# A causal attention kernel whose first pair of heads per batch goes up the blocks of queries, with the near pieces of its bias table loaded during the projections

## The chip, the cores and the metric

The kernel runs on one core of one Trainium2 chip. The metric is the device time of one execution in microseconds (us); lower is better. The engines are called as in the profile: PE (TensorE, matrix multiply; PEld is its weight load), DVE (VectorE), ACT (ScalarE), POOL (GpSimd) and SP (SyncE, which issues most of the DMAs here; SPq is its queue).

## The reference, cut to what matters

Two batches of 2048 tokens with 512 features go through one attention layer with 16 heads of 64 that share one key and one value head, and then through a feed-forward layer with ternary weights. Only the attention matters for the change:

```python
q = l2norm((xn @ Wq) per head) * q_scale
k = l2norm(xn @ Wk) * k_scale            # one key head for all 16
sim = 8.0 * q @ k.T + bias[i - j]        # relative position bias from a small network
sim = where(j <= i, sim, -inf)           # causal; a null key with its own bias stays visible
out = softmax(sim) @ [null_v, v]
```

Everything is held to float32 accuracy by splitting values into a high and a low half of 16 bits.

## The kernel before, in words

Each batch has three stages, written for every engine as `project`, `attend` and `output`. In `project` the 16 tiles of 128 tokens go through a pipeline of stages with lags: normalise, split, turn by DMA (`turn_x`), multiply by the weights on PE (L1255), square, sum, root, scale (`b_unit`, L1020, writes `qn`), take the high half on ACT (`b_high`, L716) and the low half on POOL (`b_low`, L562), and turn the pair of halves by DMA into `qT` (`turn_q`, L420). Keys and values take a shorter way: `b_turn_k` (L1267) turns the keys of a tile on PE, and `b_keys` on ACT (L727) copies them into `kT`; `b_turn_v`, `b_vhigh` and `b_values` (L1041) make the values. `output` of the first batch overlaps the first steps of the second batch's `project`.

`attend` works on 8 pairs of heads (`hp`). In a pair the queries are cut into 4 blocks `i` of 512, and a unit is a block `i` with a tile `j` of 128 keys, `j` from 0 to 4i+3: 4, 8, 12 and 16 units, `NU` = 40 in all. The last four units of a block lie on the diagonal and are 4, 3, 2 and 1 quarters wide. `BLOCKS` is 3, 2, 1, 0, so every pair goes down: block 3 with its 16 units first. Each unit goes through these engines in order:

- PE, `score` (L1286, L1289): 4 matmuls of up to 512 columns into two of four PSUM banks, so unit k waits until unit k-2 is biased.
- DVE, `bias` (L1058): scale, add the bias table, write `probs`, a ring of 10 (`RING`).
- ACT, `exps` (L749): Exp in place.
- POOL, `low_part` (L577): the low half, a ring of 8 (`LRING`). Units with `j` = 3 off the diagonal (3 of 40, `WHOLE`) have no low part; they are weighed in float32 (L1308).
- PE, `weigh` (L1322): multiplies probabilities with values into sums, in three parts that come 6, 8 and 9 slots behind `score` (`LAG`, `LATE`).

At a block's end ACT makes the null key's part (`null_part`, L756, 8 instructions), DVE drains the three sums (`drain`, L1077, L1079; its first part waits for the null part), and ACT stores the result (`store_o`, L765, 8 instructions). When these come is set by the dictionaries `NULLS`, `DRAINS` and `STORES`, by slot.

The bias table of a pair sits in `tab`, two heads of 2048 columns, loaded from DRAM in four pieces of 512 columns (L436), each waiting for the landing of the one before. Block `i` tile `j` reads 512 columns from 512i - 128j on, so block 3 begins with piece 3 and soon needs piece 2, and block 0 needs piece 0 alone. `tab` is shared with the projections' buffers: pieces 0 and 1 lie where `x_re` (the output stage's reload of x) and `xhl` (the split input of `turn_x`) are, pieces 2 and 3 where `x_in` and `xT` are. `probs`, `low` and `null_tmp` share `work` with the projections' `rest`, `sq`, `khl`, `qn` and `qhl`.

Order around the change: each engine's instructions stand in one stream. On PE, `attend` comes behind `b_turn_k` of the last tile and begins with waits for all keys, all values, `b_pn` and all of `turn_q`. On SP, `attend` comes behind the last `turn_q`. On ACT, `attend` begins with the Exp of `p_null` (L781), which loads the Exp table of functions, and `b_pn` then lets POOL begin.

## Time and profile before

| | us |
|---|---|
| median of 3 runs | 1564.64 |
| lowest, highest | 1559.87, 1564.86 |
| the profiled execution's own time | 1564.24 |
| its span in the trace | 1562.5 |
| mean granted TensorE clock | 0.971 |

The profiled execution is 0.40 us under the median, and 1.74 us of it lie outside the span. Busy shares of the span are PE 92%, PEld 60%, DVE 77%, ACT 67% and POOL 81%. The share is a mean over stages: in the forty slices of the page POOL is at 9 tenths or more through the attention of both batches and at 4 to 7 in the other stages.

### The profile page before, as it was taken

The numbers are of one execution on the slowest core, as the hardware profiler recorded it, in microseconds if no ns is written. First come the engines' busy times: TensorE is split into PE (matmuls) and PEld (weight loads), VectorE is DVE, ScalarE is ACT, GpSimd is POOL, SyncE is SP. The second block draws the span as 40 slices with busy tenths as digits, with TensorE's granted clock in tenths as the row PEclk, the third lists the DMA queues.
The fourth block names the chain that finished last, engine by engine and source line by source line (L and its number), as shares of the span: only waits on it lengthen the run. The fifth ranks groups of instructions, "written<-read, shape, count | busy, mean of one in ns | idle before, by whom it ended". The sixth has DMA issues, their size and how long they took to land.

```text
span 1562.5 us, 39526 instructions
## 1 busy us (share of the span) xinstructions
PE 1434.3 (92%) x13844; PEld 935.6 (60%) x13844; DVE 1199.8 (77%) x2071; ACT 1041.8 (67%) x2140; POOL 1262.5 (81%) x908
## 2 busy tenths in 40 slices
PE   4888995999999999997997995999999999997996
PEld 2444552777777777774443552777777777776442
DVE  4455885788788788784997885788888888886797
ACT  4664654889888888886112563788888888888110
POOL 4564755999999999997653663999999999999553
PEclk9999996999999999998999997999999999999998
DMA  7003874111211201201885885111111121110796
GB/s 213 1 1 72 176 146 84 44 27 42 47 24 42 48 23 42 51 6 30 173 189 142 159 164 105 41 42 42 29 42 42 29 42 42 29 29 5 143 192 148
DMA packets 225620, 114.93 MB, mean 74 GB/s; under 512 B 193200, under 2 KB 193712, under 8 KB 225456
## 3 DMA queue, kind: packets, MB, share of 16 engines
q1 hardware_dynamic: 220864, 104.42, 31.9%
q10 hardware_dynamic: 4608, 8.39, 1.5%
q8 instruction: 110, 1.80, 0.5%
q14 instruction: 38, 0.31, 0.1%
HBM read 58.11 MB, written 8.54 MB: 43 GB/s over the span
## 4 chain that ended last, share of the span: by engine, by line
PE 58%; POOL 11%; issue 9%; DVE 7%; DMA 3%; ACT 2%; SPq 1%; DVEq 0%; POOLq 0%; ACTq 0%
PE ps L1322 15%; PE ps L1286 12%; PE ps L1289 11%; PE ps L1255 10%; POOL work L577 7%; PE ps L1361 4%; PE ps L1308 4%; DVE work L1058 4%; POOL work L590 2%; DMA work<-work 1%; DMA tab<-bias_table 1%; POOL work L607 1%; SPq L452 1%; DVE work L1077 1%; PE ps L1370 1%
## 5 line engine op out<-in xcount | busy, mean ns | idle before, releaser
L577 POOL TENSOR_TENSOR work<-work 128x1024 f16<-128x1024 f32 (+3 forms) x592 | 932.6, 1624 | 28.5 <-ACT work L749 28.5
L1058 DVE SCALAR_TENSOR_TENSOR work<-ps,tab 128x1024 f32<-128x1024 f32 (+3 forms) x640 | 668.5, 1057 | 171.6 <-PE ps L1289 140.1
L749 ACT ACTIVATE work<-work 128x1024 f32<-128x1024 f32 (+3 forms) x640 | 572.9, 922 | 157.5 <-DVE work L1058 152.9
L1322 PEld LDWEIGHTS ps<-vals,work 128*128 128x128 bf16 (+1 forms) x7936 | 435.4, 99 | 108.6 <-POOL work L577 6.7
L1322 PE MATMUL ps<-vals,work 128*128 128x129 f16 (+1 forms) x7936 | 460.8, 207 | 4.0 <-POOL work L577 3.1
L1286 PE MATMUL ps<-qo,kT 128*128 128x512 f16 (+3 forms) x1280 | 345.5, 352 | 30.3 <-DVE work L1058 15.9
L1289 PE MATMUL ps<-qo,kT 128*128 128x512 f16 (+3 forms) x1280 | 344.6, 351 | 0.0
L1289 PEld LDWEIGHTS ps<-qo,kT 128*128 128x128 f16 x1280 | 123.4, 99 | 119.3 <-issue 6.3
L1361 PE MATMUL ps<-wout,work 128*128 128x512 f16 x768 | 174.0, 385 | 18.2 <-DMA work<-work 18.2
L1255 PE MATMUL ps<-wq,tab 128*128 128x512 f16 x768 | 177.3, 381 | 0.4
L1361 PEld LDWEIGHTS ps<-wout,work 128*128 128x128 f16 x768 | 75.9, 99 | 111.7 <-DMA work<-work 18.4
L765 ACT ACTIVATE qo<-work,rec 128x64 f32 (+1 forms) x512 | 128.4, 333 | 3.5 <-DVE rec L1082 3.5
L756 ACT ACTIVATE work<-null_v,p_null 128x65 f32<-128x65 f32 x512 | 128.7, 334 | 0.0
L797 ACT CAST work<-qo 128x1024 f16<-128x1024 f32 x32 | 33.4, 1045 | 138.3 <-DMA work<-work 138.2
L1255 PEld LDWEIGHTS ps<-wq,tab 128*128 128x128 f16 x768 | 74.8, 101 | 78.0 <-issue 2.7
L1286 PEld LDWEIGHTS ps<-qo,kT 128*128 128x128 f16 x1280 | 84.8, 99 | 47.9 <-DVE work L1058 30.9
L1308 PE MATMUL ps<-vals_w,work 128*128 128x65 f32 x768 | 109.1, 275 | 0.0
L1308 PEld LDWEIGHTS ps<-vals_w,work 128*128 128x128 f32 x768 | 100.6, 192 | 6.6
L598 POOL TENSOR_TENSOR rstd<-ve,minus_half 128x1 f32<-128x1 f32 x32 | 17.5, 548 | 82.6 <-DVE ve L1116 82.6
L590 POOL TENSOR_TENSOR work<-qo,work 128x1024 f16<-128x1024 f32 x32 | 68.0, 2126 | 12.5 <-ACT work L797 12.5
L1077 DVE TENSOR_TENSOR work<-ps,work 128x195 f32<-128x195 f32 (+1 forms) x192 | 63.1, 329 | 18.2 <-PE ps L1322 17.8
L567 POOL TENSOR_TENSOR tab<-tab 128x512 f16<-128x512 f32 x32 | 37.0, 1157 | 47.7 <-ACT tab L682 47.7
(135 smaller groups left out, 1276.3 us busy)
## 6 DMA issues: line engine op xcount, KB each, us to landing
tab<-bias_table SPq DMA_DIRECT2D x64, 512.0 KB, 4.6
tab<-in_x SPq DMA_DIRECT2D x64, 256.0 KB, 3.1
out_x<-work ACTq DMA_DIRECT2D x32, 256.0 KB, 2.3
work<-in_L_cond_Wq SPq DMA_DIRECT2D x1, 2048.0 KB, 8.7
work<-in_L_cond_Wout SPq DMA_DIRECT2D x2, 1024.0 KB, 10.2
qo<-in_L_cond_w SPq DMA_DIRECT2D x1, 1024.0 KB, 7.3
work<-work SPq DMA_TRANSPOSE x64, 4.3
qo<-in_L_cond_b SPq DMA_DIRECT2D x2, 256.0 KB, 5.4
```

The source lines that it names most:

```text
L577: pool.tensor_tensor(low[:, k % LRING, :, c0:512], probs[:, r, :, c0:512], high[:, r, :, c0:512], ALU.subtract).then_inc(low_pool, 1)
L590: pool.tensor_tensor(o_hl[:, u, 1, :].rearrange("p (h d) -> p h d", d=DH), o_all[:, :, tile, :], o_hl[:, u, 0, :].rearrange("p (h d) -> p ...
L749: act.activation(probs[:, k % RING, :, c0:512], probs[:, k % RING, :, c0:512], ACT.Exp).then_inc(expd, 1)
L756: last = act.activation(null_tmp[:, i % 2, t, :], null_v[:, :], ACT.Copy, scale=p_null[:, 4 * i + t // 2, bass.ds(2 * hp + t % 2, 1)])
L765: last = act.activation(o_all[:, bass.ds(2 * hp + t % 2, 1), 4 * i + t // 2, :].squeeze(1), o_sum[:, i % 2, t, :], ACT.Copy, scale=rec[:, ...
L1058: dve.scalar_tensor_tensor(out=probs[:, k % RING, :, c0:512], in0=ps[:, 2 * (k % 2):2 * (k % 2) + 2, c0:512], scalar=SCORE, in1=tab[:, :, ...
L1255: last = pe.matmul(ps[:, bank, 0:w], xT[:, u, rows, c, :], right, start=k == c == 0, stop=k == len(PASSES) - 1 and c == KC - 1)
L1286: pe.matmul(ps[:, 2 * (k % 2) + e, c0:512], kT[:, 0, j * P:(j + 1) * P], qT[:, 2 * hp + e, 512 * i + c0:512 * i + 512], start=True, stop=F ...
L1289: last = pe.matmul(ps[:, 2 * (k % 2) + e, c0:512], kT[:, 1, j * P:(j + 1) * P], qT[:, 2 * hp + e, 512 * i + c0:512 * i + 512], start=False ...
L1308: last = pe.matmul(ps[:, sum_bank(i, q), (t % SUMS) * VS:(t % SUMS) * VS + VW], probs[:, rings[0], t % 2, (t // 2) * P:(t // 2 + 1) * P], ...
L1322: last = pe.matmul(ps[:, sum_bank(i, q), (t % SUMS) * VS:(t % SUMS) * VS + w], parts[:, rings[part], e, s * P:(s + 1) * P], vals[:, j, 0:w ...
L1361: last = pe.matmul(ps[:, 2 + u, :], oT[:, u, rows, c, :], wout[:, cols, c, :], start=k == c == 0, stop=k == len(PASSES) - 1 and c == 2 * K ...
```

## The change

`BLOCKS`, `UNITS` and what follows from them become a class `Order`, with two instances. `DOWN` is the old order. `UP` takes the blocks as 0, 1, 2, 3 and is used by the first pair of each batch; its null part for block 0 comes after unit 6. The three weighing parts stay as they were. The places of `probs` are shifted by `FIRST` = 4, so the first units of the batch write to places 4 to 9, which the last projections do not use. PE's waits at the start are moved to the units that need them (`ready`), and the last tile's `b_turn_k` comes after the scores of units 0 and 1. SP loads table pieces 0 and 1 in the projections' step of the last tile with lag 3, that is in its stream behind `turn_q` of tile 12 and ahead of `turn_q` of tiles 13, 14 and 15, and pieces 2 and 3 behind the last `turn_q`. The second pair is written out beside the first, and the loop runs from the third (on POOL from the second).

```diff
+FIRST = 4
+class Order:
+    def __init__(self, blocks, first_null):
+        self.blocks = tuple(blocks)
+        self.units = [(i, j) for i in self.blocks for j in range(4 * i + 4)]
+        at = self.units.index
...
+        self.nulls = {at((i, 4 * i + 1)): i for i in self.blocks[1:]}
+        self.nulls[first_null] = self.blocks[0]
...
+UP = Order(range(NB), 6)
+DOWN = Order(reversed(range(NB)), 4 * NB - 3)
...
+                def first_table(i):
+                    sp.wait_ge(tab_ld, 16 * (b * HP * NB + i) + 16)
+                    alone(sp)
+                    sp.dma_start(tab[:, :, 512 * i:512 * i + 512],
+                                 bass.AP(table.tensor, 1 + P + 512 * i, [[1, P], [TABW, 2], [1, 512]])).then_inc(tab_ld, 16)
+
+                def first_tables(t, u):
+                    if t != NT - 1:
+                        return
+
+                    sp.wait_ge(table_stored, 16)
+                    for u in range(2):
+                        sp.wait_ge(b_xd[u], 16 * (NT // 2) * (b + 1))
+                    sp.wait_ge(c_xb, NT * b + 2)
+                    first_table(0)
+                    first_table(1)
...
                 def attend():
-                    sp.wait_ge(table_stored, 16)
 
                     for n in range(3):
                         sp.wait_ge(b_proj[n], NT * (b + 1))
...
+                    first_table(2)
+                    first_table(3)
+                    for i in DOWN.blocks:
+
+                        table_piece(1, i, UP.units.index((NB - 1, 4 * (NB - 1 - i) + 3)))
+                    with sp.Fori(2, HP) as hp:
+                        for i in DOWN.blocks:
+                            table_piece(hp, i, DOWN.units.index((i, 4 * i + 3)))
...
-                return [(load_x, 0), (turn_q, 6), (turn_x, 1)], attend, [(turn_y, 4), (reload_x, 3), (turn_o, 0)]
+                return [(load_x, 0), (turn_q, 6), (turn_x, 1), (first_tables, 3)], attend, [(turn_y, 4), (reload_x, 3), (turn_o, 0)]
...
+                    pool.wait_ge(b_lo, NT * (b + 1))
+                    for k in UP.pool_low:
+                        low_part(0, UP, k)
+                    with pool.Fori(1, HP) as hp:
+                        for k in DOWN.pool_low:
+                            low_part(hp, DOWN, k)
...
+                def null_part(hp, order, i):
+                    turn = order.turn(i)
+                    m = (b * HP + hp) * NB + turn
                     act.wait_ge(o_added, 3 * m + 3)
+                    if order is UP and turn == 0:
+                        act.wait_ge(b_pn, b + 1)
+
+                        for u in range(2):
+                            act.wait_ge(b_qd[u], 16 * (NT // 2) * (b + 1))
...
-                    heads(0, True)
-                    with act.Fori(1, HP) as hp:
-                        heads(hp, False)
+                    heads(0, UP, None)
+                    heads(1, DOWN, UP)
+                    with act.Fori(2, HP) as hp:
+                        heads(hp, DOWN, DOWN)
...
+                    if order is UP and j == 0:
+                        dve.wait_ge(tab_ld, 16 * (before + i + 1) + 16)
+                    elif order is DOWN and i == NB - 1 and j in NEARER:
+
+                        dve.wait_ge(tab_ld, 16 * (before + NEARER.index(j) + 1) + 16)
+                    if order is UP and FIRST + k == RING:
+
+                        dve.wait_ge(b_turned, NT * (b + 1) + 2)
...
+                def b_turn_keys(t, u):
+
+                    if t < NT - 1:
+                        b_turn_k(t, u)
+
...
-                project = [(b_project(2), 3), (b_project(1), 3), (b_turn_v, 4), (b_project(0), 3), (b_turn_k, 5)]
-
-                def score(hp, k):
+                project = [(b_project(2), 3), (b_project(1), 3), (b_turn_v, 4), (b_project(0), 3), (b_turn_keys, 5)]
+
+                def ready(k):
+
+                    i, j, c0 = UP.unit(k)
+                    if k < 2:
+
+                        pe.wait_ge(b_qn, NT * (b + 1) + 1 + k)
+                    if j == 0:
+                        pe.wait_ge(b_cd, NT * b + 4 * i + 4 + 1)
+                        pe.wait_ge(b_vl, NT * b + 4 * i + 4 + 1)
+                        for u in range(2):
+                            pe.wait_ge(b_qd[u], 16 * (NT // 2 * b + 2 * i + 2))
+                    if k == 0:
+                        pe.wait_ge(ones_set, b + 1)
+                        pe.wait_ge(b_vw, 2 * len(WHOLE_KEYS) * (b + 1))
...
                 def attend():
-                    pe.wait_ge(b_cd, NT * (b + 1) + 1)
-                    pe.wait_ge(b_vl, NT * (b + 1) + 1)
-                    pe.wait_ge(ones_set, b + 1)
-                    pe.wait_ge(b_vw, 2 * len(WHOLE_KEYS) * (b + 1))
-                    pe.wait_ge(b_pn, b + 1)
-                    for u in range(2):
-                        pe.wait_ge(b_qd[u], 16 * (NT // 2) * (b + 1))
                     for hp in range(HP):
+                        order, behind = ((UP, None), (DOWN, UP), (DOWN, DOWN))[min(hp, 2)]
                         for k in range(NU):
-                            score(hp, k)
-                            weigh_slot(hp, k)
+                            score(hp, order, k)
+                            if hp == 0 and k == 1:
+                                b_turn_k(NT - 1, (NT - 1) % 2)
+                            weigh_slot(hp, order, behind, k)
```

## Rows read from the trace of the kernel before

**Rows 1.** The page, part 1: busy time of each engine.

```profile
PE 1434.3 (92%) x13844; PEld 935.6 (60%) x13844; DVE 1199.8 (77%) x2071; ACT 1041.8 (67%) x2140; POOL 1262.5 (81%) x908
```

**Rows 2.** Windows table: length, busy (instructions) PE, PEld, DVE, ACT, POOL; clock, DMA, GB/s.

```profile
256.00:314.00 58.00, 56.53 (x646) 40.28 (x647) 45.98 (x57) 45.70 (x86) 54.49 (x34) 0.94 0.23 52
...
372.70:431.00 58.30, 57.67 (x710) 42.76 (x709) 48.40 (x69) 50.55 (x105) 58.30 (x39) 1.00 0.17 37
```

**Rows 3.** Waits, whole span: who waited for whom, total us, times, longest.

```profile
DVE work L1058 <- DMA tab<-bias_table: 28.7, 4, 11.0
...
POOL work L577 <- ACT work L749: 28.5, 6, 10.4
```

**Rows 4.** Timeline of POOL, first batch: start, us, instruction, [idle before, releaser].

```profile
253.69 1.89 POOL L577 TENSOR_TENSOR work<-work 128x1024 f16<-128x1024 f32 x1 [10.44 <-ACT work L749]
258.33 3.74 POOL L577 TENSOR_TENSOR work<-work 128x1024 f16<-128x1024 f32 x2 [2.75 <-ACT work L749]
263.25 23.40 POOL L577 TENSOR_TENSOR work<-work 128x1024 f16<-128x1024 f32 x14 [1.17 <-ACT work L749]
```

**Rows 5.** Chain that ended last, 226 to 275 us: start, us, what.

```profile
243.28 2.00 SPq L420
...
245.98 5.04 DMA tab<-bias_table
...
251.24 4.59 DMA tab<-bias_table
```

**Rows 6.** Timeline of PE around the first batch's start of attention.

```profile
238.38 0.37 PE L1267 MATMUL ps<-flip,work 128*128 128x128 f16 x2 [4.38 <-DVE vals L1041]
241.23 0.39 PE L1267 MATMUL ps<-flip,work 128*128 128x128 f16 x2 [2.48 <-POOL work L557]
247.81 1.01 PE L1286 MATMUL ps<-qo,kT 128*128 128x512 f16 x2 [6.19 <-DMA qo<-work]
...
257.14 1.04 PE L1286 MATMUL ps<-qo,kT 128*128 128x512 f16 x2 [2.77 <-DVE work L1058]
...
258.82 1.06 PE L1286 MATMUL ps<-qo,kT 128*128 128x512 f16 x2
```

**Rows 7.** Timeline of DVE, its last operation before the first unit.

```profile
239.78 0.42 DVE L1095 SCALAR_TENSOR_TENSOR p_null<-p_null,null_shift 128x256 f32<-128x256 f32 x1
```

**Rows 8.** Timeline of ACT, from the last tile's high half to the first null part.

```profile
239.42 1.04 ACT L716 CAST work<-work 128x1024 f16<-128x1024 f32 x1 [0.27 <-DVE work L1020]
...
241.66 0.37 ACT L727 CAST kT<-ps 128x256 f16<-128x256 f32 x1 [0.99 <-PE ps L1267]
242.05 1.28 ACT L781 ACT_TABLE_LOAD   x1
243.34 0.42 ACT L781 ACTIVATE p_null<-p_null 128x256 f32<-128x256 f32 x1
...
276.27 2.01 ACT L756 ACTIVATE work<-null_v,p_null 128x65 f32<-128x65 f32 x8
```

**Rows 9.** Timeline of SP: the issues of `turn_q` for tiles 12 and 13.

```profile
224.91 1.93 SPq L420 DMA_TRANSPOSE qo<-work  x1
231.13 1.77 SPq L420 DMA_TRANSPOSE qo<-work  x1
```

**Rows 10.** Windows of 1 us: the granted clock is the third number from the end.

```profile
261.00:262.00 1.00, 1.00 (x4) 0.26 (x2) 1.00 (x1) 0.39 (x1) 1.00 (x1) 0.50 0.06 18
262.00:263.00 1.00, 1.00 (x5) 0.45 (x4) 0.46 (x1) 0.97 (x1) 0.08 (x1) 0.73 0.85 188
```

**Rows 11.** Groups by line and form, 300 to 660 us: busy us, mean ns | idle before.

```profile
L577 POOL TENSOR_TENSOR work<-work 128x1024 f16<-128x1024 f32 x154 | 286.4, 1900 | 0.0
L1058 DVE SCALAR_TENSOR_TENSOR work<-ps,tab 128x1024 f32<-128x1024 f32 x172 | 207.5, 1218 | 42.8 <-PE ps L1289 42.2
L749 ACT ACTIVATE work<-work 128x1024 f32<-128x1024 f32 x173 | 178.5, 1052 | 46.0 <-DVE work L1058 44.7
...
L577 POOL TENSOR_TENSOR work<-work 128x256 f16<-128x256 f32 x25 | 15.5, 619 | 0.0
```

More of the change, by code:

```diff
@@ L62 @@
 HP = H // 2
-BLOCKS = tuple(reversed(range(NB)))
-UNITS = [(i, j) for i in BLOCKS for j in range(4 * i + 4)]
-NU = len(UNITS)
+NU = sum(4 * i + 4 for i in range(NB))
 RING = 10
@@ L85 @@
 WHOLE_KEYS = (3,)
-WHOLE = tuple(k for k, (i, j) in enumerate(UNITS) if j in WHOLE_KEYS and j < 4 * i)
-POOL_LOW = tuple(k for k in range(NU) if k not in WHOLE)
 SUMS = 3
@@ L93, with unit, turn, bank @@
 LATE = (0, 2, 3)
-NULLS = {UNITS.index((i, 4 * i + 1)): i for i in BLOCKS}
-DRAINS = {}
-for i, q in itertools.product(BLOCKS, range(3)):
-    DRAINS[max([UNITS.index((i, 4 * i + 1 + q)) + LAG + LATE[q] + 1] + [slot + 1 for slot in DRAINS])] = (i, q)
-STORES = {UNITS.index((i, 4 * i + 3)) + LAG + LATE[2] + 2: i for i in BLOCKS}
-def unit(k):
-    i, j = UNITS[k]
-    return i, j, P * max(0, j - 4 * i)
-def turn(i):
-    return NB - 1 - i
-def sum_bank(i, q):
-    return 4 + (SUMS * turn(i) + q) % 4
+class Order:
[3 more added lines that the diff above has]
+        at = self.units.index
+        self.whole = tuple(k for k, (i, j) in enumerate(self.units) if j in WHOLE_KEYS and j < 4 * i)
+        self.pool_low = tuple(k for k in range(NU) if k not in self.whole)
+        self.nulls = {at((i, 4 * i + 1)): i for i in self.blocks[1:]}
+        self.nulls[first_null] = self.blocks[0]
+        self.drains = {}
+        for i, q in itertools.product(self.blocks, range(3)):
+            self.drains[max([at((i, 4 * i + 1 + q)) + LAG + LATE[q] + 1] + [slot + 1 for slot in self.drains])] = (i, q)
+        self.stores = {at((i, 4 * i + 3)) + LAG + LATE[2] + 2: i for i in self.blocks}
+    def unit(self, k):
+        i, j = self.units[k]
+        return i, j, P * max(0, j - 4 * i)
+    def turn(self, i):
+        return self.blocks.index(i)
+    def bank(self, i, q):
+        return 4 + (SUMS * self.turn(i) + q) % 4
+UP = Order(range(NB), 6)
+DOWN = Order(reversed(range(NB)), 4 * NB - 3)
 def since(eng, semaphore, count):
@@ L423, in attend, with table_piece @@
+                def table_piece(hp, i, last):
+                    sp.wait_ge(biased, (b * HP + hp - 1) * NU + last + 1 + CB)
+                    sp.wait_ge(tab_ld, 16 * ((b * HP + hp) * NB + DOWN.turn(i)) + 16)
+                    alone(sp)
+                    src = bass.AP(table.tensor, hp * (2 * TABW) + 1 + P + 512 * i, [[1, P], [TABW, 2], [1, 512]])
+                    sp.dma_start(tab[:, :, 512 * i:512 * i + 512], src).then_inc(tab_ld, 16)
                 def attend():
-                    sp.wait_ge(table_stored, 16)
@@ L1099, in attend @@
                         dve.wait_ge(c_out[u], 16 * (NT // 2) * b + 16)
-                    heads(0, True)
-                    with dve.Fori(1, HP) as hp:
-                        heads(hp, False)
-                    for k in sorted(DRAINS):
+                    heads(0, UP, None)
+                    heads(1, DOWN, UP)
+                    with dve.Fori(2, HP) as hp:
+                        heads(hp, DOWN, DOWN)
+                    for k in sorted(DOWN.drains):
                         if k >= NU:
-                            drain(HP - 1, *DRAINS[k])
+                            drain(HP - 1, DOWN, *DOWN.drains[k])
                 def c_stat(t, u):
```

123 lines of the change are left out of this document (57 added, 66 removed).

## The prediction

> **What bounds the kernel now.** I read the busy times first, then windows by stage, then the waits, then the timelines where attention starts.
>
> The page's busy line names PE, at 92% [rows 1]. That is an average over stages. The windows say more. In a pair of heads that runs undisturbed, 58.3 us long, POOL is busy for all 58.3 us and PE for 57.67, a number that counts the modelled tails of matmuls [rows 2]. The groups by form agree: POOL's low part has 0.0 us of idle time before it over 360 us, while DVE waits 42.8 us for PE and ACT 46.0 us for DVE [rows 11]. Those two wait because PE's slots move with the rings that POOL empties. So **POOL's chain of low parts sets the pace of attention**: 37 low parts a pair, 58.3 us, 8 pairs a batch. In the whole execution POOL waits 28.5 us for an Exp, and in only six places [rows 3].
>
> Three of the six are seen in the first batch [rows 4]: 10.44 us before the first low part at 253.69, 2.75 before the second and 1.17 before the fourth. After 263.25 POOL never stops again. The sum is 14.36 us; the other 14.1 belong to the second batch. The end of a batch's attention is therefore the start of its first low part, plus 8 times 58.3, plus the idle time after the first one. I call 253.69 + 2.75 + 1.17 = **257.61 POOL's effective start**. Nothing else in the stage has to be timed.
>
> What makes it so late? The chain runs through the last turn of q (issued at 243.28), table piece 3 (issued 245.98, landed 5.04 us later) and piece 2 (251.24, 4.59 us) [rows 5]. DVE waits 28.7 us for table pieces in four places, two a batch, the longest 11.0 [rows 3]. PE waits 6.19 us for the turn of q before its first score at 247.81, and its third slot has to wait again until 257.14 [rows 6]. DVE itself was ready at 239.78 + 0.42 = 240.2 [rows 7], and ACT at 243.34 + 0.42 = 243.76 [rows 8].
>
> **The change part by part.** All of it lies between about 227 us and the first units of the pair, in each batch.
>
> *Start of the scores.* Block 0 needs keys and queries of tiles 0 to 3 only, so PE no longer waits for the last turns of q. Its stream reaches unit 0 behind the keys of tile 14, which start at 238.38 behind the values of tile 15 and take about 0.3 us to issue [rows 6]. A score of full width takes 258.82 - 257.14 = 1.68 us at half clock [rows 6]. So unit 0 is scored by about 240.4, unit 1 (three quarters) by 241.7.
>
> *The last keys, moved.* `b_turn_k` of tile 15 now stands behind these two scores: it starts near 241.7 instead of 241.23 [rows 6], so what follows on ACT is about 0.45 us late. Behind it are the copy of the keys, the load of the Exp table (1.28 us) and the Exp of `p_null` (0.42), which ran from 241.66 to 243.76 [rows 8]. I get ACT free at 244.2. DVE is not in the way: unit 0 is biased by 240.6 + 1.22 = 241.8 and unit 1 by 242.8 [rows 7, 11].
>
> *First low part.* ACT's first Exp runs 1.05 us from 244.2 [rows 11], and POOL follows at about **245.4**, where it started at 253.69 before [rows 4]. The new bound of the start is ACT's table load, no longer the DMAs.
>
> *Table pieces 0 and 1.* SP has them behind `turn_q` of tile 12, issued at 224.91 for 1.93 us [rows 9]. Piece 0 then goes out near 227.2 and lands by 227.2 + 5.0 = 232.2, piece 1 by 232.4 + 4.6 = 237.0 [rows 5]. Unit 0 wants piece 0 at 240.6 and unit 4 wants piece 1 at about 245.6: hidden by 8 us each. What is queued behind them is `turn_q` of tile 13, whose issue slips from 231.13 [rows 9] to about 232.8, as SP waits for piece 0 to land. ACT waits for that turn before it takes the high half of tile 15, at 239.42 [rows 8]. A turn took about 247.81 - 243.28 = 4.5 us from its issue to its reader [rows 5, 6], so it lands at 237.3, in time. Were it to stand fully behind piece 1's 4.6 us as well, it would land at 241.9, 2.5 us late, and that would go one for one into POOL's start. I take 0, since the nearest row is a piece that was issued 2.7 us behind a turn, with both in flight: it took 5.04 instead of 4.59 us, a slip of 0.45 us and not of a whole transfer [rows 5]. The Trainium skill's page "DMA: Bandwidth & Descriptors", section "Queues, rings and completion order", says that each DMA engine consumes a ring's descriptors in order. By that rule the turn's data would come behind piece 1, and my estimate is 0.6 us late; no row here shows a turn behind a piece.
>
> *Table pieces 2 and 3* stay where the old first two were, landing at about 251 and 256 [rows 5]. Units 12 and 24 want them near 258 and 278. Hidden.
>
> *The walk up.* Is POOL fed once it has started? The units of block 0 give it 1.86 us for a full one (286.4 / 154) and 0.57 for a quarter, its mean of 0.62 less the overlap of neighbours [rows 11]; with the two between, 4.9 us, to 250.3. ACT has 2.8 us of Exp for these four and is through at 247.0. Units 4, 5 and 6 are scored at half clock, one per 1.7 us, from 243.8 on, so they are biased at 246.8, 248.5 and 250.2, and ACT is through with unit 6 at 251.3. Then comes the null part of block 0, 2.0 us [rows 8], to 253.3. DVE's first drain is at slot 8 and waits for it; it takes 0.7 us, the bias of unit 8 then 1.2, its Exp 1.05, so low part 8 can start at 256.2. POOL is through with units 4, 5 and 6 at 250.3 + 3 x 1.86 = 255.9, and unit 7 has no low part. That is 0.3 to 0.5 us of idle time. Between units 13 and 16 ACT has three Exps (one of a unit without a low part) and the store of block 0, 5.1 us, against 3.7 us of POOL's; its lead of 1 us is used up and about 0.5 us of idle time comes again. After that ACT has 2.0 us blocks only with more full units between them. I take **1.0 us** of idle time in the pair, with 0 below (POOL goes without a gap for the rest of the stage) and, above, the 3.9 us that it had after its first low part before [rows 4].
>
> *Sum.* The effective start goes from 257.61 to 245.4 + 1.0 = 246.4, or 11.2 us earlier. The other seven pairs, the tail and the output stage are the same work in the same order. The second batch starts attention in the same way (28.5 and 28.7 us of waits are two times 14.3) [rows 3], so 22.4 us for both. Written-out code for one more pair on ACT, DVE and POOL I cost at 0: the first pair was written out before, and POOL shows no gap where the loop begins. Against the profiled execution's own time 1564.24 - 22.4 = **1541.8**; that execution is 0.4 us under the median of the runs, so the same number stands for a median.
>
> **The rivals.**
>
> *Starved on the way up.* The narrow units come first, when the pipeline has no stock, and two null parts, a store and six drains fall into units 6 to 16. If each of these three ACT blocks of 2.0 us stops POOL in full instead of being covered, POOL idles 6 us instead of 1.0, and the gain is 6.2 us a batch: 1564.2 - 12.4 = 1551.8. For it: ACT is at 50.55 of 58.30 us even in an undisturbed pair [rows 2], and the drain couples DVE to it. Against it: each block falls where POOL has 1 to 2.5 us of work in stock by my walk. A late turn of tile 13 (2.5 us) ends near the same place.
>
> *PE stays at the lower clock: slower than before.* After the gap at 241 to 247 us PE worked at 0.50 of full speed, the 1.2 GHz level, until it had been at work without a break from 257.14 to about 262.5; then the clock rose to 2.4 GHz [rows 6, 10]. On the way up PE has less to do: a slot costs about 1 us at full clock in units 4 to 11, against 1.2 to 1.9 of the others, so its work is patchy. If the clock stayed low, a slot of steady state would cost 2 x 57.67 / 40 = 2.9 us [rows 2], against 58.3 / 40 = 1.46 for POOL. Each slot loses 1.4 us, so the gain of 11.2 us is used up after 8 such slots, some 23 us, and from there the change is slower. Over half a pair it loses 28 us and is 17 us slower a batch: 1598. Against it: at half clock PE's work doubles, so the patches close by themselves, which is what raised the clock before, and the first window of 58 us with its cold start still shows a mean of 0.94 [rows 2]. The skill's page "TensorE: Matmul & The Clock Gate", section "A second HAM failure mode: psum-queue depth-cycling", describes a kernel that cycles through PSUM banks with small gaps and goes back and forth between the two levels. By that rule the way up would be such a case; the trace shows 1.00 through the steady pairs, which cycle through the same banks [rows 2].
>
> *Not what it says.* Another wait could stand where the table's stood: for instance the null part of block 0 waits for all turns of q, which land at 247.8 [rows 6]; by my walk ACT comes there at 251.3. If something of this kind holds POOL until 253 or so, the change is worth nothing: 1562 to 1565.
>
> **How the numbers follow.** About 0.3% (4.7 us) can be told from no change here. The forecast has 0.70: with idle time 0 and the start at 245.0, 12.6 us a batch, 1539; with 3.9 us of idle time, 8.3 us a batch, 1547.6. Starvation or the late turn has 0.17, at 1548 to 1556, still faster. Nothing gained has 0.06, slower 0.07. Faster by over 0.3% is 0.70 + 0.17 = 0.87, within 0.3% is 0.06, slower 0.07. The range reaches from 1538 to 1552, which holds the forecast's case and the nearer half of the starved one.
>
> **What would show it.** Right: the first L577 near 245.4 and not at 253.7; POOL's waits for ACT shrink from 28.5 to about 6 us; DVE's wait for table pieces is gone; the first score is at about 238.7; the pairs after the first still take 58.3 us. Wrong in a step: the first low part later than 246.5 with ACT's L716 waiting for a DMA (the late turn); waits of L577 for L749 around units 8 and 16 of over 2 us (starved); a granted clock of 0.50 past about 250 us. If the first low part is early and the end of attention is not, the claim that POOL alone sets the pace is wrong.

## The result, and the profile after

| | before | after |
|---|---|---|
| median of the runs, us | 1563.18 (4 runs) | 1540.23 (4 runs) |
| lowest, highest | 1559.87, 1564.86 | 1536.95, 1541.57 |
| profiled execution, own time | 1564.24 | 1539.39 |
| its span | 1562.5 | 1537.2 |
| mean granted TensorE clock | 0.971 | 0.983 |

The ratio is 0.9851, with a 95% interval of 0.9837 to 0.9866: 22.95 us between the medians. The forecast was 1541.8 and a gain of 22.4; between the two profiled executions, by which it was worked out, the gain is 24.85. The busy times of the page hardly move against [rows 1]. The same work is done in less time:

```profile
span 1537.2 us, 39074 instructions
...
PE 1427.8 (93%) x13844; PEld 933.7 (61%) x13844; DVE 1200.2 (78%) x2071; ACT 1041.3 (68%) x2140; POOL 1264.0 (82%) x908
```

Where the time went stands in the timeline of POOL. These are its low parts (now L610) in the first and in the second batch; the columns are start, us, instruction, and idle time before it with its releaser:

```profile
245.07 466.47 POOL L610 TENSOR_TENSOR work<-work 128x1024 f16<-128x1024 f32 x296 [2.13 <-ACT work L786]
...
947.42 466.60 POOL L610 TENSOR_TENSOR work<-work 128x1024 f16<-128x1024 f32 x296 [2.13 <-ACT work L786]
```

One group a batch: 296 low parts, 8 times 58.3 us, without a gap. Before, the first one stood at 253.69 and two gaps came behind it [rows 4]. The waits of the whole span say the same. POOL's 28.5 us for an Exp [rows 3] are now 4.3, DVE's 28.7 us for the table are gone, and a small new wait stands beside them, DVE for the null part:

```profile
POOL work L610 <- ACT work L786: 4.3, 2, 2.1
...
DVE work L1128 <- ACT work L798: 3.9, 2, 2.0
```

**A common clock for all kernels.** The last projection matmul ends at a slightly different time in every execution, so starts are counted from it. Before, it ended at 232.13; here it ends at 229.05 + 2.75 = 231.80 in this timeline of PE, which goes on to the first scores:

```profile
229.05 2.75 PE L1307 MATMUL ps<-wq,tab 128*128 128x512 f16 x12
...
238.05 0.37 PE L1319 MATMUL ps<-flip,work 128*128 128x128 f16 x2 [4.38 <-DVE vals L1085]
238.50 1.01 PE L1360 MATMUL ps<-qo,kT 128*128 128x512 f16 x2
...
241.44 0.42 PE L1319 MATMUL ps<-flip,work 128*128 128x128 f16 x2
241.88 0.39 PE L1360 MATMUL ps<-qo,kT 128*128 128x256 f16 x2
...
253.28 0.39 PE L1360 MATMUL ps<-qo,kT 128*128 128x256 f16 x2 [2.41 <-DVE work L1108]
```

The first score starts right behind tile 14's keys, and tile 15's keys (the second L1319) stand behind unit 1, as written. POOL's effective start (first low part plus all idle time behind it) was 21.56 + 2.75 + 1.17 = 25.48 us behind the last projection and is now 245.07 - 231.80 = 13.27. That is 12.2 us less. The second batch went from 25.29 to 13.28, 12.0 less. Together it is 24.2 of the 24.85 us between the two profiled executions.

ACT from the last high half (L752) on:

```profile
239.10 1.05 ACT L752 CAST work<-work 128x1024 f16<-128x1024 f32 x1 [0.27 <-DVE work L1064]
...
241.89 0.37 ACT L763 CAST kT<-ps 128x256 f16<-128x256 f32 x1 [1.55 <-PE ps L1319]
242.28 1.28 ACT L824 ACT_TABLE_LOAD   x1
243.58 0.42 ACT L824 ACTIVATE p_null<-p_null 128x256 f32<-128x256 f32 x1
243.90 5.44 ACT L786 ACTIVATE work<-work 128x1024 f32<-128x1024 f32 x7
249.25 2.01 ACT L798 ACTIVATE work<-null_v,p_null 128x65 f32<-128x65 f32 x8
...
261.85 2.00 ACT L808 ACTIVATE qo<-work,rec 128x64 f32<-128x64 f32 x8
263.76 3.08 ACT L786 ACTIVATE work<-work 128x1024 f32<-128x1024 f32 x3
```

ACT is free at 244.00 and POOL begins 1.07 us later: the load of the Exp table now stands in the chain that bounds the start, behind the copy of tile 15's keys. DVE had biased units 0 to 3 from 240.60 on. SP's timeline shows the two table pieces (L436) between the turns of tiles 12 and 13 (L430):

```profile
224.59 1.89 SPq L430 DMA_TRANSPOSE qo<-work  x1
226.74 5.64 SPq L436 DMA_DIRECT2D tab<-bias_table  x2
232.43 12.43 SPq L430 DMA_TRANSPOSE qo<-work  x3
```

The turn of tile 13 went out at 232.43, 1.6 us later than in [rows 9] when both are counted from the last projection. The table of DMA issues gives it 6.4 us from issue to landing, and 5.9 us to the turn of tile 14; before the change each of the two took 4.3 us. It landed near 238.8, and ACT took the high half of tile 15 at 239.1.

The windows table (length, then busy time and instructions of PE, PEld, DVE, ACT, POOL; clock, DMA share, GB/s) shows two stretches at the start of attention and the two of [rows 2]:

```profile
240.00:242.00 2.00, 1.97 (x8) 0.85 (x7) 1.40 (x2) 0.45 (x3) 1.58 (x2) 0.56 0.71 135
242.00:244.00 2.00, 1.46 (x11) 0.74 (x10) 1.62 (x3) 1.97 (x4) 0.94 (x1) 1.00 0.00 0
256.00:314.00 58.00, 58.00 (x700) 42.34 (x698) 48.23 (x63) 47.40 (x85) 58.00 (x36) 1.00 0.17 38
372.70:431.00 58.30, 57.56 (x708) 42.59 (x706) 48.33 (x68) 50.28 (x106) 58.30 (x38) 1.00 0.17 38
```

The steady pair is unchanged at 58.3 us of POOL. TensorE was granted its full clock from about 241.8 on, after PE had worked almost without a break from 238.05.

### The profile page after: what moved, and what is told of

It is laid out like the page before. It is cut to its first block, busy times and chain, and to the rows that moved or that the text cites. A ratio compares the mean times of both kernels' runs of the same rounds, so it can differ in the third digit from the quotient of the medians.

```text
span 1537.2 us, 39074 instructions
## 1 busy us (share of the span) xinstructions
PE 1427.8 (93%) x13844; PEld 933.7 (61%) x13844; DVE 1200.2 (78%) x2071; ACT 1041.3 (68%) x2140; POOL 1264.0 (82%) x908
## 4 chain that ended last, share of the span: by engine, by line
PE 57%; POOL 13%; issue 10%; DVE 7%; ACT 3%; DMA 2%; SPq 1%; DVEq 0%; POOLq 0%; ACTq 0%
PE ps L1396 15%; PE ps L1360 12%; PE ps L1363 11%; PE ps L1307 10%; POOL work L610 8%; PE ps L1382 4%; DVE work L1108 3%; POOL work L626 3%; PE ps L1431 2%; POOL work L643 2%; ACT work L786 1%; DMA work<-work 1%; DVE work L1128 1%; DMA tab<-in_x 1%; SPq L485 1%
## 5 line engine op out<-in xcount | busy, mean ns | idle before, releaser
L610 POOL TENSOR_TENSOR work<-work 128x1024 f16<-128x1024 f32 (+3 forms) x592 | 933.0, 1620 | 4.3 <-ACT work L786 4.3
```

The costliest lines, as they stand in the source:

```text
L610: pool.tensor_tensor(low[:, k % LRING, :, c0:512], probs[:, r, :, c0:512], high[:, r, :, c0:512], ALU.subtract).then_inc(low_pool, 1)
```

## The experiments

All of them are read by one measure. "Start" is the first low part behind the last projection matmul, "idle" POOL's idle time after it, both for batch 1 / batch 2; the sum adds all four. "Rest" is the median less the sum.

| run | start | idle | sum | median | ratio to before [95%] | rest |
|---|---|---|---|---|---|---|
| before | 21.56 / 21.34 | 3.92 / 3.95 | 50.8 | 1564.5 | | 1513.7 |
| after | 13.27 / 13.28 | 0 / 0 | 26.6 | 1540.23 | 0.9851 [0.9837, 0.9866] | 1513.7 |
| e1 order only | 22.67 / 21.78 | 4.65 / 5.15 | 54.3 | 1566.04 | 1.0002 [0.9990, 1.0014] | 1511.8 |
| e2 pieces only | 21.30 / 20.29 | 0 / 0 | 41.6 | 1554.46 | 0.9936 [0.9913, 0.9959] | 1512.9 |
| e3 keys first | 14.09 / 14.36 | 1.82 / 3.76 | 34.0 | 1545.07 | 0.9870 [0.9847, 0.9894] | 1511.0 |
| e4 Exp table early | 10.91 / 11.54 | 1.23 / 0.96 | 24.6 | 1538.36 | 0.9839 [0.9814, 0.9863] | 1513.8 |
| e5 null parts longer | 13.27 / 13.28 | 3.01 / 2.99 | 32.6 | 1546.77 | 0.9890 [0.9868, 0.9912] | 1514.2 |
| e6 = e4, null part a slot earlier | 11.06 / 11.35 | 0.17 / 0 | 22.6 | 1535.37 | 0.9812 [0.9793, 0.9830] | 1512.8 |
| e7 = e6, store at slot 17 | 10.93 / 11.46 | 0.35 / 0.31 | 23.1 | 1536.57 | 0.9821 [0.9805, 0.9838] | 1513.5 |
| e8 sum in another form | 13.28 / 13.28 | 0 / 1.71 | 28.3 | 1542.91 | 0.9862 [0.9844, 0.9879] | 1514.6 |
| e9 pieces behind turn 13 | 13.31 / 13.37 | 0.31 / 1.88 | 28.9 | 1541.67 | 0.9848 [0.9830, 0.9867] | 1512.8 |
| e10 = e6 with e9 | 10.91 / 10.90 | 1.92 / 0.99 | 24.7 | 1537.35 | 0.9827 [0.9809, 0.9845] | 1512.6 |
| e11 = e10 with e8 | 10.90 / 10.91 | 1.73 / 1.15 | 24.7 | 1535.88 | 0.9827 [0.9804, 0.9850] | 1511.2 |
| e12 root in PSUM | 14.45 / 12.89 | 0.99 / 2.01 | 30.3 | 1544.00 | 0.9858 [0.9830, 0.9885] | 1513.7 |

**The last column is the first finding.** Over fourteen kernels the sum goes from 22.6 to 54.3 us and the median less the sum stays within 1511.0 to 1514.6. A straight line through the fourteen points has a slope of 0.99: one microsecond of POOL's effective start is one microsecond of the kernel. This holds to some 3 us and not finer. The sum comes from one execution and the median from several; with each profiled execution's own time the rest lies within 1510.0 to 1514.6 in twelve kernels, at 1507.9 in e6 and at 1517.9 in e1, whose profiled executions were the fastest of five and the slowest of ten. The median "before" in the row is that of the later runs beside e1 to e4 (1564.52).

### e1 and e2: one half of the change at a time

e1 keeps the walk up and takes the early pieces away:

```diff
-                    first_table(2)
-                    first_table(3)
+                    sp.wait_ge(table_stored, 16)
+                    for i in range(4):
+                        first_table(i)
...
-... (turn_x, 1), (first_tables, 3)], attend, ...
+... (turn_x, 1)], attend, ...
```

> The changed kernel with only the way up: all four table pieces are loaded behind the last turn of q, as before the change. Theory S (the end of attention follows the effective start of POOL's low parts one for one): piece 0 is issued near 245.6 and lands near 250.6, unit 0 is biased by 251.9, the first low part starts near 253.1 instead of 245.07, with up to 0.5 us of idle time after it, so the effective start is 253.1 to 253.6, 8 to 8.5 us later than in the changed kernel and about 4 us earlier than before the change (257.61). Time 1556 to 1558. Rival O (the narrow units first are what gains, since they fill the pipeline; the table's place matters little): under 1549.

e2 is the kernel before, going down, with pieces 3 and 2 loaded one lag later and 1 and 0 behind the last turn:

```diff
+                def first_tables(t, u):
+                    if t != NT - 1:
+                        return
+                    for n in range(3):
+                        sp.wait_ge(b_proj[n], NT * (b + 1))
+                    first_table(3)
+                    first_table(2)
...
+... (turn_x, 1), (first_tables, 4)], attend, ...
```

> The kernel before with only the early table: the pairs all go down, and pieces 3 and 2 are loaded behind the turn of tile 13, once the projections are through. Theory S: PE still waits for the last turn of q and starts its scores near 247.5; unit 0 is biased by 250.7, the first low part starts near 251.8; PE is at half clock, so POOL waits about 1.2 us again near unit 4. Effective start near 253, 4.6 us earlier than before, time near 1554 to 1556. The two halves alone would then gain about 4 and 4.6 us a batch, and together 12.3, as each alone leaves the other's wait. Rival D (the DMAs of the table were the whole delay and the order is beside the point): as fast as the changed kernel, near 1540.

The order alone is worth nothing and the pieces alone 10 us, while both together give 23. Neither half alone gives the start its 8 us, because each leaves one late producer in front of DVE. In e2 the late one is the last turn of q: PE waits 7.21 us for it before its first score. POOL's gaps behind the first low part are gone, though: of its 10 us these gaps are 7.9 (3.9 + 4.0) and the start 1.3 (0.3 + 1.05). In e1 it is the table. Its DVE waited 12.14 us for piece 0 and 1.77 for piece 1; the chain that ended last (start, us, what) shows piece 0 slower than the 5.04 of [rows 5]. In both a turn had gone out shortly before, 2.2 us ahead here and 2.7 there; whether this makes the difference is not shown:

```profile
246.04 6.67 DMA tab<-bias_table
```

e1 also shows what I had feared of the way up. PE had stood idle for 11.42 us and came back at the 1.2 GHz level. Windows and POOL's timeline of e1:

```profile
256.00:258.00 2.00, 1.91 (x5) 0.73 (x6) 0.28 (x1) 0.92 (x2) 2.00 (x2) 0.50 0.24 66
```

```profile
255.34 4.89 POOL L611 TENSOR_TENSOR work<-work 128x1024 f16<-128x1024 f32 x4 [11.54 <-ACT work L787]
260.45 5.59 POOL L611 TENSOR_TENSOR work<-work 128x1024 f16<-128x1024 f32 x3 [0.21 <-ACT work L787]
268.21 4.89 POOL L611 TENSOR_TENSOR work<-work 128x1024 f16<-128x1024 f32 x4 [2.17 <-ACT work L787]
```

The way up idles 4.65 and 5.15 us here, against 0 in the changed kernel and 0 in e2, which goes down. My expectation of about 4 us a batch for the order alone was wrong: the start came 0.5 to 1.4 us later than expected and the idle time was 4.65 and 5.15 us instead of at most 0.5. The way up was dear where it started late and at the lower clock; which of the two does it, no run separates.

### e3: the last keys ahead of the scores

```diff
-... (b_project(0), 3), (b_turn_keys, 5)]
+... (b_project(0), 3), (b_turn_k, 5)]
...
-                            if hp == 0 and k == 1:
-                                b_turn_k(NT - 1, (NT - 1) % 2)
```

> The changed kernel with the turn of the last tile's keys back ahead of unit 0's score. Theory S: PE turns them near 240.9, unit 0's score ends near 243.0 at half clock and its Exp near 245.4; first low part near 245.5, 0.5 us later than in the changed kernel. As PE starts later its clock rises later too, and POOL may wait up to 1 us near units 4 to 8. 1 to 3 us slower in all, 1541 to 1543. Rival (the place of this turn decides when PE may begin at all): 5 us slower or more.

The median is 4.8 us up, more than was expected; by the ratios to the kernel before it is 3.0 us, with overlapping intervals. The start is only 0.8 and 1.1 us later; the greater part is idle time on the way up, 1.82 and 3.76. The sum of the profiled execution is 7.5 us up and its own time 6.9 (1546.24 against 1539.39), so the 4.8 us of the median are the less certain figure.

### e4 and e5: is there stock on the way up?

e4 moves the load of the Exp table into a place where ACT waits, by one dummy Exp behind the last square root:

```diff
+        spare = sb("spare", [P, 1], F32)
...
+                    if t == NT - 1:
+                        act.activation(spare[:, :], mask_r[:, 0:1], ACT.Exp)
```

> The changed kernel with one Exp of a single column on ACT right behind the last Sqrt of a batch, so that the load of the Exp table of functions falls into a gap of ACT. Its result is not used. The first low part should start 1.28 us earlier, near 243.8. Theory S in its plain form (the start is all): 1.2 us a batch faster, 2.5 us in all. Theory S with the slack read from the changed kernel's trace: the Exp of unit 16 ends at 265.83 there and POOL is free for it at 265.87, a slack of 0.04 us, and that Exp hangs on the null part of block 0, which hangs on the bias of unit 6 and not on the table; so POOL idles about 1.2 us near unit 16, and only 0 to 0.3 us a batch are gained: the same time as the changed kernel within 1 us.

The start comes 2.36 and 1.74 us earlier, and 1.23 and 0.96 us of it, about half, are given back as idle time on the way up. The median, 1538.36, is 1.9 us below that of the changed kernel, but the intervals overlap; the loss of half of the start's gain is read from the trace, not from the time.

e5 lengthens the null parts of blocks 0 and 1 in the first pair by eight narrow operations:

```diff
+                    if order is UP and turn < 2:
+                        for t in range(8):
+                            act.activation(spare[:, 8 * turn + t, :], null_v[:, 0:8], ACT.Copy,
+                                           scale=p_null[:, 4 * i + t // 2, bass.ds(2 * hp + t % 2, 1)])
```

> The changed kernel with eight more short instructions on ACT (8 columns wide, into a spare tile that nobody reads) ahead of the null parts of blocks 0 and 1 of the first pair, some 1.6 us each. Theory S with the slack as read from the changed kernel's trace: the chain null part of block 0, first drain, bias of unit 8, its Exp has 1.2 us to spare at unit 8 and about 0.04 us at unit 16. So POOL, which has no idle time on the way up in the changed kernel, idles about 1.6 us in each batch, most of it by unit 16, and perhaps as much again from the second null part: 3 to 6 us slower in all, 1543 to 1546. Rival (the way up has slack, as my own walk had it, with 1 to 2.5 us in stock before each block of ACT work): under 1 us slower.

ACT's timeline of e5 shows the added 1.63 us, and POOL's what became of them:

```profile
250.19 1.63 ACT L800 ACTIVATE spare<-null_v,p_null 128x8 f32<-128x8 f32 x8
```

```profile
256.87 3.32 POOL L611 TENSOR_TENSOR work<-work 128x1024 f16<-128x1024 f32 x2 [0.42 <-ACT work L787]
261.57 7.17 POOL L611 TENSOR_TENSOR work<-work 128x512 f16<-128x512 f32 x5 [1.39 <-ACT work L787]
269.94 61.15 POOL L611 TENSOR_TENSOR work<-work 128x1024 f16<-128x1024 f32 x36 [1.20 <-ACT work L787]
```

These are the same places in the changed kernel, ACT's Exps of units 8 and 9 and POOL's low parts of units 6 and 8, the second of which begins at 255.5 (timelines of 252 to 256 and of 255 to 257 us):

```profile
253.26 1.79 ACT L786 ACTIVATE work<-work 128x1024 f32<-128x1024 f32 x2 [1.06 <-DVE work L1108]
```

```profile
253.63 3.75 POOL L610 TENSOR_TENSOR work<-work 128x1024 f16<-128x1024 f32 x2
```

The Exp of unit 8 was done at 254.3 and POOL was free for it at 255.5, a slack of 1.2 us. 1.63 - 1.2 = 0.4 us, and 0.42 is seen. At unit 16 it was 265.83 against 265.87, no slack at all. Of 2 x 2 x 1.63 = 6.5 us of added ACT work 6.0 come out as idle time of POOL, and the median is 6.5 us up. The rival (slack on the whole way up, under 1 us slower) fell: the stock is 1.2 us at unit 8 and is used up by unit 16. One thing blurs the size: in both starts of e5 the clock of TensorE also dipped (told below), which it did not in the changed kernel, and DVE waited 2.04 us for PE at 260.20. Part of the 1.2 us at unit 16 may be the dip's.

### e6 and e7: the null part a slot earlier, the store later

If the null part of block 0 is what the way up stumbles over, it should come before ACT has fallen behind. e6 is e4 with it after unit 5, and e7 also stores block 0 one slot later, at 17:

```diff
-UP = Order(range(NB), 6)
+UP = Order(range(NB), 5)
```

> The kernel of e4 with block 0's null part after unit 5 instead of 6. In e4 the low parts start 0.1 to 0.2 us behind POOL's last projection work and then idle 0.25 and 0.98 us (first batch) and 0.96 us (second). Theory S: the null part starts about 1.2 us earlier, DVE's wait of 1.97 us for it shrinks to under 1, and POOL's idle time at units 8 and 16 goes: 0 to 0.4 us a batch. Time 1.0 to 2.4 us under e4's. Rival (the idle time at unit 16 comes from the store of block 0 after unit 14 alone, and moving the null part does nothing for it): within 0.5 us of e4.

> The kernel of e6 with the store of block 0 after unit 17 instead of 14 in the first pair, so that ACT's 2.0 us for it no longer stand ahead of the Exps of units 15, 16 and 17. Theory S: POOL's idle time after its first low part is 0 in both batches; not slower than e6, at most 0.5 us a batch faster. Rival (the later store holds up a drain or a later Exp, as the units ahead of the next narrow ones have no slack): idle time of over 1 us comes at units 18 to 24.

POOL's timeline of e6, both batches:

```profile
240.94 20.86 POOL L611 TENSOR_TENSOR work<-work 128x1024 f16<-128x1024 f32 x14 [0.16 <-ACT work L789]
261.96 445.65 POOL L611 TENSOR_TENSOR work<-work 128x1024 f16<-128x1024 f32 x282 [0.17 <-ACT work L789]
...
938.63 466.57 POOL L611 TENSOR_TENSOR work<-work 128x1024 f16<-128x1024 f32 x296
```

The start kept e4's gain and the idle time is down to 0.17 us and 0. **e6 has the lowest median of all, 1535.37**, 4.9 us below the changed kernel's, and its interval of the ratio (up to 0.9830) ends below the other's (from 0.9837). In e7 0.35 and 0.31 us of idle time are left, where I had expected none; the store's place makes no difference that these runs can tell.

### e8 to e12: what else stands in front of the start

The chain of the changed kernel has one odd link, a sum of 17 columns on DVE (`twice`) that takes 178 ns by the median of 32 and 2.05 us for the last tiles. In the changed kernel's timelines of DVE and of POOL it ends with POOL's low part of tile 14:

```profile
235.47 2.04 DVE L1053 TENSOR_TENSOR twice<-quot,root 128x17 f32<-128x17 f32 x1
```

```profile
235.36 2.12 POOL L595 TENSOR_TENSOR work<-work 128x1024 f16<-128x1024 f32 x1
```

One theory blamed the form of the instruction (e8), another two inputs from SBUF while POOL runs (e12, which puts `root` of the last tile into PSUM). A third held that the turn of tile 13 should not stand behind the pieces (e9). e10 and e11 put these parts together with e6.

```diff
e8
-                    dve.tensor_tensor(twice[:, :], quot[:, :], root[:, u, :], ALU.add).then_inc(b_near, 1)
+                    dve.scalar_tensor_tensor(out=twice[:, :], in0=quot[:, :], scalar=1.0, in1=root[:, u, :], op0=ALU.mult,
+                                             op1=ALU.add).then_inc(b_near, 1)
e9, e10, e11
-... (turn_x, 1), (first_tables, 3)], attend, ...
+... (turn_x, 1), (first_tables, 4)], attend, ...
e12
+        def root_of(t, u):
+            return ps[:, 6, 448:448 + H + 1] if t == NT - 1 else root[:, u, :]
...
-                    dve.tensor_tensor(twice[:, :], quot[:, :], root[:, u, :], ALU.add).then_inc(b_near, 1)
+                    dve.tensor_tensor(twice[:, :], quot[:, :], root_of(t, u), ALU.add).then_inc(b_near, 1)
```

> The changed kernel with one DVE instruction in another form: twice = quot + root, 17 columns, written as quot * 1.0 + root (scalar_tensor_tensor instead of tensor_tensor). In the changed kernel's trace it takes 178 ns in most tiles and 2.05 us in the last ones, where it ends just as POOL's low half of tile 14 ends. Theory L (this form is held while POOL works, and the other form, in which the bias runs beside POOL at 1.22 us, is not): it takes about 0.2 us, so tile 15's qn comes 1.85 us earlier. But ACT's high half of tile 15 then waits for the turn of tile 13, which stands behind table piece 1: it landed near 238.7 where ACT would want it at 237.3 (after the change's own clock of the trace). So that wait goes to about 1.5 us and only about 0.4 us a batch are gained, 1539 to 1540. Rival (the 2.05 us are something else's): the instruction stays at 2 us and nothing moves.

> The changed kernel with table pieces 0 and 1 one step later in SP's stream, behind the turn of tile 13 and ahead of that of tile 14. Theory S: piece 0 goes out near 233.2 and lands near 238, in time for unit 0 at 240.6; piece 1 lands near 242.7, in time for unit 4 at 244.5. Same time as the changed kernel within 1 us, first low part 13.3 us behind the last projection as there. Rival (pieces need the slack that the earlier place gives): DVE waits for a table piece, 1 us or more slower.

> The kernel of e6 with the table pieces behind the turn of tile 13. In e6 ACT waited 0.98 and 1.46 us for the turn of tile 13 before the high half of tile 15, with the low parts starting 11.1 to 11.4 us behind the last projection. Theory Q (that turn was late because piece 1 was ahead of it): the wait goes to 0.3 or less, the low parts start 0.5 to 1 us earlier, 1 to 2 us in all under e6. Rival (ACT then waits for DVE's qn instead, which is due at the same time): within 0.5 us of e6.

> The kernel of e10 with the sum of e8 in its other form. Theories S, L and Q together: POOL's low half of tile 15 ends 1.5 to 1.85 us earlier after the last projection than in e10 (near 9 us instead of 10.5 to 11), and the low parts follow at once. Idle time on the way up may come back by up to 1 us, since piece 1 lands near 242.7 and unit 4 wants it near 242.5. 1 to 3.5 us under e10.

> The changed kernel with the last tile's roots (17 columns) written by ACT to PSUM instead of SBUF, so that the DVE sum twice = quot + root has one input in SBUF and one in PSUM. Theory P (a DVE instruction with two SBUF inputs is held while POOL works, one with a PSUM input is not, as the bias is not held at 1.22 us): the sum of tile 15 takes 0.2 us instead of 2.05, and tile 15's qn comes 1.8 us earlier. ACT's high half of tile 15 then waits for the turn of tile 13, which lands about 6.9 to 7.6 us behind the last projection behind table piece 1: a wait for the DMA of 1 to 2 us appears, and the low parts start only 0 to 0.6 us earlier. Time 1539 to 1541, no difference that can be told. Rival (the hold has nothing to do with where the inputs lie): the sum stays at 2.05 us and nothing moves.

**The form is not it.** In e8 the new instruction takes 178 ns by the median and 2053 at most, as the old one. **The place of the input is.** DVE and POOL in e12:

```profile
236.71 0.17 DVE L1056 TENSOR_TENSOR twice<-quot,ps 128x17 f32<-128x17 f32 x1
```

```profile
236.60 2.12 POOL L598 TENSOR_TENSOR work<-work 128x1024 f16<-128x1024 f32 x1
```

It runs from start to end while POOL's operation is under way, in both batches, and its form is the old one. The 1.9 us did not reach the end, because the next thing was late. In e12 ACT waited 3.88 and 2.42 us for the turn of tile 13, which took 8.14 and 6.6 us behind the table pieces, and the start was 1.2 us later in one batch and 0.4 earlier in the other. Why this turn took 8.14 us here and 6.4 in the changed kernel, in the same place of the queue, is not shown. ACT's timeline, and the chain that ended last:

```profile
242.08 1.04 ACT L755 CAST work<-work 128x1024 f16<-128x1024 f32 x1 [3.88 <-DMA qo<-work]
```

```profile
233.86 8.14 DMA qo<-work
```

**The pieces behind the turn** (e9) cost and gained nothing that the median can tell, but the expectation that piece 1 lands in time was wrong: DVE waited 1.39 us for it in the first batch. On top of e6 (e10) ACT's wait for the turn went from 0.98 and 1.46 us to nothing, and 1.92 and 0.99 us of idle time came in its place on the way up; 1537.35 is not told apart from e6. DVE waited 1.66 us for piece 1 in e10 and 1.38 in e11, and ACT's null part 0.94 and 0.95 us for the last turns of q. These two waits took the place of ACT's. The theory behind e10 was right for the wait and wrong for the time. In e11 the sum's form could give nothing: with the Exp table loaded early the sum of the last tile takes 0.18 us already in e4, e6, e7 and e10.

**A dip of the clock, found by reading across the runs.** Windows of 1 us were read over the first 30 us or so of attention in both batches of every kernel. Twelve kernels walk up, 24 starts in all. In 8 of them the granted clock fell from 2.4 back to 1.2 GHz for 3 to 4 us on the way up: both batches of e1 and e5, and batch 2 of e3, e8, e9 and e12. (In e1 it had been low before that as well, in the first batch from its gap of 11.42 us on until 259 us.) The windows of e8, batch 2:

```profile
955.00:956.00 1.00, 0.00 (x0) 0.00 (x0) 1.00 (x2) 0.26 (x1) 1.00 (x1) 1.00 0.84 188
956.00:957.00 1.00, 0.66 (x5) 0.51 (x6) 1.00 (x2) 0.68 (x1) 1.00 (x2) 0.78 0.80 174
957.00:959.00 2.00, 2.00 (x25) 2.00 (x24) 1.72 (x5) 2.00 (x7) 2.00 (x2) 0.50 0.39 89
959.00:960.00 1.00, 1.00 (x10) 0.68 (x8) 0.23 (x1) 1.00 (x6) 1.00 (x1) 0.51 0.00 0
960.00:961.00 1.00, 1.00 (x15) 0.65 (x13) 0.20 (x1) 0.85 (x3) 1.00 (x2) 1.00 0.00 0
```

and what POOL and PE show there:

```profile
970.50 59.76 POOL L610 TENSOR_TENSOR work<-work 128x1024 f16<-128x1024 f32 x35 [1.71 <-ACT work L786]
```

```profile
956.34 0.43 PE L1361 MATMUL ps<-qo,kT 128*128 128x256 f16 x2 [2.58 <-DVE work L1109]
```

PE had just been idle for 2.58 us: its slot waited for DVE, DVE for the null part. POOL then starves at unit 16 for 1.71 us. That same 1.71 stands at unit 16 in every one of these starts outside e5 (which has 1.20), and in none of the other 16 (0 to 0.99). The gap of PE ahead of the dip was 2.49 to 2.59 us, and 3.95 in e5. The changed kernel has the same idle time of PE (2.41, and 2.58 in batch 2) without the dip, and so have both batches of e4 and the first of e3, e8, e9 and e12, so the idle time alone does not decide it. In e6 the null part comes a slot earlier and PE's gap is 1.30 and 1.52 us; in the 8 starts of e6, e7, e10 and e11, with gaps of 1.30 to 2.36, the clock never fell. That is a pattern across runs, not an experiment made for it.

## Why the prediction was right, and where it was not

- *POOL's effective start decides, and nothing else in the stage has to be timed.* Right, one for one over fourteen kernels, to within some 3 us.
- *Start of the scores, moved keys, bias, ACT free at 244.2, first low part at 245.4.* With the trace shifted by the 0.33 us between the two last projections, the first score is at 238.83 (forecast 238.7), the bias of unit 0 at 240.93 (240.6), the moved keys at 241.77 (241.7), ACT is free at 244.33 (244.2) and POOL begins at 245.40 (245.4). The moved keys were the right thing to count. Ahead of the scores (e3) the median is 4.8 us higher, so their new place is worth more than the 0.45 us that it costs.
- *ACT's table load as the new bound.* Right. Moved (e4) it gives 2.36 and 1.74 us of start. More than its own 1.28, since the sum `twice` then no longer meets POOL's operation.
- *Pieces 0 and 1 hidden, the late turn at 0.* Right in the changed kernel, with 0.3 us to spare, and here luck had a part. The size in between was larger than the row that I leaned on: the turn behind piece 1 took 6.4 us, 1.9 more than the 4.5 of the forecast and not 0.45. Nearer rows stood in the trace of the kernel before, and I had overlooked them: turns issued 0.6 to 0.8 us behind a 256 KB load of x took from 4.4 to 8.0 us to land (6.5 for the one issued at 153.64, 8.0 for that at 872.98). Nor would a late turn go into POOL's start one for one, as I wrote. In e8 it came 0.38 and 0.55 us late for ACT and the start stayed at 13.28: the turn leads to the start by way of POOL's low half of the last keys, done at 240.85, and their turn on PE, which stands behind two scores until 241.44, so 0.6 us are hidden there. The Trainium skill's page "DMA: Bandwidth & Descriptors", section "Queues, rings and completion order", has each DMA engine work off a ring's descriptors in order; the trace agrees in so far as piece 1 landed near 237.0 and the turn issued behind it near 238.8. (The 0.6 us late that I gave for this rule has no working in the prediction.) As soon as ACT comes earlier, the wait is there: 0.90 and 1.64 us in e4, 0.98 and 1.46 in e6, 3.88 and 2.42 in e12.
- *The walk up, 1.0 us of idle time.* Off by its whole size: 0. I had PE at half clock until about 249; it worked on from 238.05, since the scores no longer waited, and had the full clock from 241.8. The null part began at 249.25 (249.58 on the forecast's clock) and not at 251.3. Over both batches that is 2.0 us, and the forecast was 1.6 us above the median and 2.4 above the profiled execution.
- *"Each block falls where POOL has 1 to 2.5 us of work in stock."* **This step was wrong**, though the number survived it. The stock was 1.2 us at unit 8 and 0.04 us at unit 16, and e5 turned 6.5 us of added ACT work into 6.0 us of idle time. That the idle time was 0 with so little in stock is luck as much as forecast.
- *The rivals.* Starvation on the way up is what e1, e3 and e5 show; the changed kernel had 0.04 us left. PE at the lower clock did not come as I had drawn it: the clock was full from 241.8. It did fall back in 8 starts of 24 of the kernels that walk up, but rose again after 3 to 4 us; the idle time that goes with it is some 1.7 us, where the rival had 28. The change did what it says.

## What to carry to other kernels

Find the engine that never idles in the steady state, and measure from the last instruction of the stage before to the moment from which it runs without a gap. That one distance, start plus the idle time behind it, is what a change at a stage's seam is worth. Remove all late producers of the first unit together: here one half of the change gave 0 us, the other 10, and both 23. When the start has been moved forward, look at how close each later block came to stopping the pacing engine (end of its input against the time it was free). A slack of 0.04 us means that the next gain is given back there unless that block is moved too.

## What the runs showed of the hardware

- A DVE operation of 17 columns with both inputs in SBUF takes 0.18 us alone and 2.04 us when POOL is in a two-input operation of 2.12 us, and ends within 0.05 us of POOL's. With one input in PSUM it takes 0.17 us beside it (e12, two instances). The Trainium skill's page "SBUF — State Buffer", section "SBUF: two separate sides", describes a port pair that DVE and GpSimd share as an exclusive lock, held for a whole instruction; e12 agrees with it.
- A turn by DMA took 4.3 us from issue to landing for the last tiles before the change, 6.4 when issued 0.4 us behind a table piece of 512 KB in SP's queue, and 8.14 in e12. A piece took 4.6 us by the median of the page before; issued 2.7 and 2.2 us behind a turn, it took 5.04 (before) and 6.67 (e1).
- The granted clock can fall for 3 to 4 us in a kernel that is dense on average, after a gap of 2.5 to 2.6 us in PE's work, and doesn't do so each time: six starts had it with the dip and six with a gap of 2.49 to 2.59 without.

Left open: whether the dip decides the scatter of the changed kernel's runs (1536.95 to 1541.57), since only one execution of each kernel was profiled; what makes the clock fall in one start and not in another with the same gap; and whether e6, e7, e10 and e11 differ at all, as their intervals overlap.
